# An LSTM step with one tanh for all four gates and its waits in another order, and the attention's output bias added behind the first two batches' sums

## The reference

```
h   = LSTM(norm(x)), 56 steps, 20 units:
      i, f, g, o = split(x_t @ W_ih.T + b_ih + b_hh + h @ W_hh.T)
      c = sigmoid(f) * c + sigmoid(i) * tanh(g)
      h = sigmoid(o) * tanh(c)
mu_w  = relu(h @ W_mu.T + b_mu);  sigma = sigmoid(h @ W_sig.T + b_sig)
mu_t  = mu_w[0] * mu_{t-1} + mu_w[1] / 56 + mu_w[2] * (t + 1) / 56
w     = exp(-(rel - mu)^2 / (2 sigma^2)), masked causally, normalised
x1    = x + w @ norm(x)
x2    = x1 + softmax(norm(x1) WQ (ctx WK)^T / 8) (ctx WV) WO + bO     16 heads of 64
out   = x2 + layer_norm(gelu(norm(x2) @ W1[e] + b1[e]) @ Wo + bo + norm(x2)) * gamma + beta, e = argmax of 4 router logits
```

## Time and profile before

| | |
|---|---|
| median of 3 executions | 1666.67 us (1659.07 to 1667.97) |
| profiled execution, its own time | 1670.2 us |
| its span in the trace | 1668.3 us |
| busy: TensorE, VectorE, ScalarE, GpSimd | 1539.9, 1169.3, 898.0, 805.3 us |
| LSTM, first input product to last head | 18.43 to 127.1 us |
| its 40 steps in the loop | 38.9 to 112 us |
| first scores | 162.28 us |

### The profile page before, as it was taken

The page is one execution under the profiler, slowest core; times in us unless marked ns, Lnnn a source line. Parts: engine busy times, 40 slices in busy tenths (PEclk is TensorE's granted clock), DMA queues, the critical chain, the costliest instruction groups (busy, mean ns, idle before and its releaser), DMA issues.

```text
span 1668.3 us, 25258 instructions
## 1 busy us (share of the span) xinstructions
PE 1539.9 (92%) x7555; PEld 1091.7 (65%) x7555; DVE 1169.3 (70%) x1870; ACT 898.0 (54%) x1281; POOL 805.3 (48%) x410
## 2 busy tenths in 40 slices
PE   6885999999999999999999999999999999989997
PEld 3345666676767676767666666666676767666574
DVE  4348777767676767686777777777767776868645
ACT  4234665555555555556565656565565555535311
POOL 2003365555555555555555555555555555536510
PEclk9996999999999999999999999999999999989898
DMA  4000000000000000000000000000000000000000
GB/s 154 26 9 10 1 37 38 38 37 37 37 37 26 37 25 37 25 37 33 37 37 37 37 37 37 37 37 37 37 37 37 37 37 37 38 5 14 1 1 22
DMA packets 15058, 54.91 MB, mean 33 GB/s; under 512 B 919, under 2 KB 6122, under 8 KB 15022
## 3 DMA queue, kind: packets, MB, share of 16 engines
q1 hardware_dynamic: 15022, 54.46, 8.6%
HBM read 53.54 MB, written 0.92 MB: 33 GB/s over the span
## 4 chain that ended last, share of the span: by engine, by line
PE 75%; DVE 12%; issue 5%; ACT 5%; POOL 1%; DVEq 1%; DMA 0%; POOLq 0%; ACTq 0%
PE ps L736 28%; PE ps L702 26%; PE ps L608 3%; PE ps L603 3%; DVE arena L1280 3%; PE ps L594 3%; PE ps L798 3%; DVE arena L1294 3%; PE ps L587 2%; PE ps L716 2%; ACT arena L996 2%; PE ps L523 1%; ACT ring L990 1%; POOL arena L456 1%; PE ps L724 1%
## 5 line engine op out<-in xcount | busy, mean ns | idle before, releaser
L456 POOL TENSOR_TENSOR arena<-arena,ring 125x896 f32<-125x896 f32 x192 | 426.0, 2219 | 17.5 <-POOL arena L456 0.5
L702 PE MATMUL ps<-q_hi,ctxT_hi 128*125 128x448 f32 x768 | 402.7, 524 | 32.7 <-ACT ring L990 26.7
L1280 DVE TENSOR_TENSOR arena<-arena,ps 125x896 f32<-125x896 f32 x336 | 363.1, 1081 | 89.6 <-PE ps L702 89.3
L456 POOL TENSOR_TENSOR arena<-arena 125x896 f32<-125x896 f32 x112 | 237.0, 2116 | 345.8 <-ACT arena L996 337.1
L990 ACT ACTIVATE ring<-ps 125x896 f32<-125x896 f32 x192 | 176.2, 918 | 380.2 <-DVE arena L1280 211.1
L736 PE MATMUL ps<-ring,ctx_nat 125*128 125x448 f32 x768 | 347.8, 549 | 0.0
L702 PE MATMUL ps<-q_hi,ctxT_lo 128*125 128x448 f32 x768 | 282.4, 368 | 0.0
L702 PE MATMUL ps<-q_lo,ctxT_hi 128*125 128x448 f32 x768 | 282.3, 368 | 0.0
L736 PE MATMUL ps<-arena,ctx_nat 125*128 125x448 f32 x576 | 243.6, 546 | 2.3
L702 PEld LDWEIGHTS ps<-q_hi,ctxT_hi 128*125 128x125 f32 x768 | 144.7, 188 | 104.7 <-issue 88.3
L1294 DVE TENSOR_TENSOR ring<-ring,ps 125x896 f32<-125x896 f32 x192 | 201.8, 1079 | 0.0
(11 more groups left out here) (203 smaller groups left out, 1936.4 us busy)
## 6 DMA issues: line engine op xcount, KB each, us to landing
ctx_raw<-in_ctx_dram SPq DMA_DIRECT2D x32, 750.0 KB
ctx_nat<-in_ctx_dram SPq DMA_DIRECT2D x32, 750.0 KB
w_sb<-in_L_ffn_W_dram SPq DMA_DIRECT2D x1, 1024.0 KB
resid<-in_x_dram SPq DMA_DIRECT2D x1, 896.0 KB, 5.9
out_dram<-ctx_raw SPq DMA_DIRECT2D x4, 224.0 KB, 2.5
ctx_raw<-in_L_xattn_WQ_dram SPq DMA_DIRECT2D x1, 512.0 KB
w_sb<-in_L_xattn_WK_dram SPq DMA_DIRECT2D x1, 512.0 KB
w_sb<-in_L_xattn_WV_dram SPq DMA_DIRECT2D x1, 512.0 KB
```

Of the source, the lines that this page charges most:

```text
L456: g.tensor_tensor(summed, chunk[0] if j == 1 else summed, chunk[j], ALU.add).then_inc(s["prob_added"], 1)
L702: m = mm(score_ps[j % 2][:, half, :], cx[k][:, rows], q[k][:, cols], start=(n == 0), stop=(n == 2))
L1280: v.tensor_tensor(run_max, kept(k, 0) if j == 1 else run_max, score_ps[j % 2], ALU.max).then_inc(s["maxed"], 1)
```

## The change

It has five parts. **One tanh.** Since sigmoid(z) = (1 + tanh(z / 2)) / 2, the weights and biases of gates i, f and o are halved when they are copied out of PSUM, and one tanh instruction covers all four gates (20 x 128). The tiles hold twice the cell and twice `h`; `W_hh` and the head's weights are halved once more for that, and the row of ones in `lstm_h` becomes 2. **Three VectorE instructions for four.** `cell` is now the fifth block behind the four gates, so one instruction computes (gate + 1) x (g or cell) for i and f together (20 x 64), a second adds the two parts, and a third makes `h`. **Waits.** VectorE's wait for its own earlier step now stands ahead of the wait for ScalarE. **Biases.** They are loaded as columns beside the weights (80, 80, 3 and 1 numbers of 4 bytes), behind the weights in the SP queue; TensorE's first transposes wait for all eight loads, and ScalarE makes seven copies instead of three. **GpSimd's order.** `bO` is added in two halves of eight tiles, behind the additions of batch 0 and of batch 1, and the heads of a pair wait for it; the three powers in period (14, 0) stand behind addition 11 together.

```diff
@@ sync
-            sp.dma_start(w_hh_in[0:4 * PE, :], W_hh).then_inc(s["lstm_w_in"], 16)
...
-            sp.dma_start(whhT[PE:PE + 1, :], b_ih.rearrange("(a n) -> a n", a=1)).then_inc(s["bias_in"], 16)
...
+            for column, bias in ((PE, b_ih), (PE + 1, b_hh)):
+                sp.dma_start(w_hh_in[0:4 * PE, column:column + 1], bias.rearrange("(n a) -> n a", a=1)).then_inc(s["lstm_w_in"], 16)
...
@@ gpsimd
-            g.memset(lstm_h, 1.0).then_inc(s["zeros_made"], 1)
+            g.memset(lstm_h, 2.0).then_inc(s["zeros_made"], 1)
...
-            need(pool, "ln_done", 2 * GROUPS)
-            g.tensor_tensor(resid_k, resid_k, bO_b[:, None, :].to_broadcast((TOK, PAIRS, D)), ALU.add).then_inc(s["bO_added"], 1)
...
-                    if isinstance(i, int) and i == PAIRS - 2 and k == 0 and j in POWERS_AT:
-                        power(3, POWERS_AT.index(j))
+                if isinstance(i, int) and i == 0:
+                    tiles = slice(k * PAIRS // 2, (k + 1) * PAIRS // 2)
+                    if k == 0:
+                        need(pool, "ln_done", 2 * GROUPS)
+                    g.tensor_tensor(resid_k[:, tiles, :], resid_k[:, tiles, :], bO_b[:, None, :].to_broadcast((TOK, PAIRS // 2, D)), ALU.add).then_inc(s["bO_added"], 1)
+                if isinstance(i, int) and i == PAIRS - 2 and k == 0:
+                    for q in range(GROUPS - 1):
+                        power(3, q)
@@ tensor
-            pe.wait_ge(s["lstm_w_in"], 64)
+            pe.wait_ge(s["lstm_w_in"], 128)
...
@@ scalar
-            a(cell_t, cell, ACT.Sigmoid).then_inc(s["table_loaded"], 1)
+            a(cell_t, cell, ACT.Tanh).then_inc(s["table_loaded"], 1)
...
+            for start, stop, half in ((0, 2 * PE, 0.5), (2 * PE, 3 * PE, 1.0), (3 * PE, 4 * PE, 0.5)):
+                a(wihT[:, start:stop], ps[:, 3, start:stop], ACT.Copy, scale=half).then_inc(s["lstm_w_sb"], 1)
+                a(whhT[0:PE + 2, start:stop], ps[0:PE + 2, 3, 128 + start:128 + stop], ACT.Copy, scale=half / 2).then_inc(s["lstm_w_sb"], 1)
...
-                    a(gate_act[:, 0:3, :], gates[:, 0:3, :], ACT.Sigmoid).then_inc(s["sig_ready"], 1)
-                    a(gate_act[:, 3, :], gates[:, 3, :], ACT.Tanh).then_inc(s["tanhg_ready"], 1)
-                    need(act, "cell_step", 3 * t + 3)
-                    a(cell_t, cell, ACT.Tanh).then_inc(s["tanhc_ready"], 1)
+                    a(gate_act[:, 0:4, :], gates, ACT.Tanh).then_inc(s["tanhg_ready"], 1)
+                    need(act, "cell_step", 2 * t + 2)
+                    a(cell_t, cell, ACT.Tanh, scale=0.5).then_inc(s["tanhc_ready"], 1)
@@ vector
-                    need(dve, "sig_ready", t + 1)
-                    need(dve, "cell_step", 3 * t)
-                    v.tensor_tensor(cell_f, gate_act[:, 1, :], cell, ALU.mult).then_inc(s["cell_step"], 1)
+                    need(dve, "cell_step", 2 * t)
                     need(dve, "tanhg_ready", t + 1)
-                    v.tensor_tensor(cell_i, gate_act[:, 0, :], gate_act[:, 3, :], ALU.mult).then_inc(s["cell_step"], 1)
-                    need(dve, "cell_step", 3 * t + 2)
-                    v.tensor_tensor(cell, cell_f, cell_i, ALU.add).then_inc(s["cell_step"], 1)
+                    v.scalar_tensor_tensor(cell_parts, gate_act[:, 0:2, :], 1.0, gate_act[:, 3:5, :], ALU.add, ALU.mult).then_inc(s["cell_step"], 1)
+                    need(dve, "cell_step", 2 * t + 1)
+                    v.scalar_tensor_tensor(cell, cell_parts[:, 1, :], 0.5, cell_parts[:, 0, :], ALU.mult, ALU.add).then_inc(s["cell_step"], 1)
                     need(dve, "tanhc_ready", t + 1)
-                    v.tensor_tensor(lstm_h[0:PE, u, :], gate_act[:, 2, :], cell_t, ALU.mult).then_inc(s["h_ready"], 1)
+                    v.scalar_tensor_tensor(lstm_h[0:PE, u, :], gate_act[:, 2, :], 1.0, cell_t, ALU.add, ALU.mult).then_inc(s["h_ready"], 1)
...
                     need(dve, "recip_done", 4 * (pair + 1))
+                    need(dve, "bO_added", 2)
...
-            need(dve, "bO_added", 1)
```

More of the change, by code:

```diff
@@ L134, in decoder_layer @@
         w_in = cut(D)
-        w_hh_in = cut(PE)
-        w_head_in = cut(PE)
+        w_hh_in = cut(PE + 2)
+        w_head_in = cut(PE + 1)
         wihT = cut(4 * PE)
@@ L139, in decoder_layer @@
         headT = cut(NB + 1)
-        gate_act = cut(4 * B, PE).rearrange("p (g b) -> p g b", g=4)
-        cell = cut(B, PE)
-        cell_f = cut(B, PE)
-        cell_i = cut(B, PE)
+        gate_act = cut(5 * B, PE).rearrange("p (g b) -> p g b", g=5)
+        cell = gate_act[:, 4, :]
+        cell_parts = cut(2 * B, PE).rearrange("p (g b) -> p g b", g=2)
         cell_t = cut(B, PE)
@@ L196, in decoder_layer @@
         s = {name: stack.enter_context(nc.semaphore("s_" + name)) for name in (
-            "x_in lstm_w_in bias_in attn_w_in ffn_w_in ctx_in0 ctx_in1 nat_in0 nat_in1 out_stored0 out_stored1 "
+            "x_in lstm_w_in attn_w_in ffn_w_in ctx_in0 ctx_in1 nat_in0 nat_in1 out_stored0 out_stored1 "
             "identity_made ones_made minus_made indices_made rel_made causal_made picks_made zeros_made "
@@ L200, in decoder_layer @@
             "ln_step ln_var rstd_done ln_done xT_ps xT_sb "
-            "gates_ready sig_ready tanhg_ready cell_step tanhc_ready h_ready head_ready head_read "
+            "gates_ready tanhg_ready cell_step tanhc_ready h_ready head_ready head_read "
             "sigma_done pick_ps picks_read gauss_step rows_picked gauss_diff gauss_sq gauss_arg gauss_exp gauss_ready gauss_w2 "
@@ L233, in decoder_layer @@
         PIECES = {"k": "mask", "x": "tokens", "l": "logits", "o": "onehot", "t": "turn", "s": "sums", "p": "project", "q": "query"}
-        POWERS_AT = (9, 10, 11)
         EARLY = 4
@@ L313, in _ @@
             sp.dma_start(w_in[0:4 * PE, :], W_ih).then_inc(s["lstm_w_in"], 16)
-            sp.dma_start(w_hh_in[0:4 * PE, :], W_hh).then_inc(s["lstm_w_in"], 16)
-            sp.dma_start(w_head_in[0:NB, :], W_mu).then_inc(s["lstm_w_in"], 16)
-            sp.dma_start(w_head_in[NB:NB + 1, :], W_sig).then_inc(s["lstm_w_in"], 16)
-            need(sp, "biased_cleared", 2)
-            sp.dma_start(headT[PE:PE + 1, 0:NB], b_mu.rearrange("(a n) -> a n", a=1)).then_inc(s["bias_in"], 16)
-            sp.dma_start(headT[PE:PE + 1, NB:NB + 1], b_sig.rearrange("(a n) -> a n", a=1)).then_inc(s["bias_in"], 16)
-            sp.dma_start(whhT[PE:PE + 1, :], b_ih.rearrange("(a n) -> a n", a=1)).then_inc(s["bias_in"], 16)
-            sp.dma_start(whhT[PE + 1:PE + 2, :], b_hh.rearrange("(a n) -> a n", a=1)).then_inc(s["bias_in"], 16)
+            sp.dma_start(w_hh_in[0:4 * PE, 0:PE], W_hh).then_inc(s["lstm_w_in"], 16)
+            sp.dma_start(w_head_in[0:NB, 0:PE], W_mu).then_inc(s["lstm_w_in"], 16)
+            sp.dma_start(w_head_in[NB:NB + 1, 0:PE], W_sig).then_inc(s["lstm_w_in"], 16)
+            for column, bias in ((PE, b_ih), (PE + 1, b_hh)):
+                sp.dma_start(w_hh_in[0:4 * PE, column:column + 1], bias.rearrange("(n a) -> n a", a=1)).then_inc(s["lstm_w_in"], 16)
+            sp.dma_start(w_head_in[0:NB, PE:PE + 1], b_mu.rearrange("(n a) -> n a", a=1)).then_inc(s["lstm_w_in"], 16)
+            sp.dma_start(w_head_in[NB:NB + 1, PE:PE + 1], b_sig.rearrange("(n a) -> n a", a=1)).then_inc(s["lstm_w_in"], 16)
             sp.dma_start(wq_raw, WQ).then_inc(s["attn_w_in"], 16)
@@ L484, in _ @@
             pe.wait_ge(s["identity_made"], 2)
-            pe.wait_ge(s["lstm_w_in"], 64)
+            pe.wait_ge(s["lstm_w_in"], 128)
             tr(ps[:, 3, 0:4 * PE], w_in[0:4 * PE, :], ident[0:4 * PE, 0:4 * PE])
-            tr(ps[0:PE, 3, 128:128 + 4 * PE], w_hh_in[0:4 * PE, :], ident[0:4 * PE, 0:4 * PE])
-            tr(ps[0:PE, 3, 256:256 + NB + 1], w_head_in[0:NB + 1, :], ident[0:NB + 1, 0:NB + 1]).then_inc(s["lstm_w_ps"], 1)
+            tr(ps[0:PE + 2, 3, 128:128 + 4 * PE], w_hh_in[0:4 * PE, :], ident[0:4 * PE, 0:4 * PE])
+            tr(ps[0:PE + 1, 3, 256:256 + NB + 1], w_head_in[0:NB + 1, :], ident[0:NB + 1, 0:NB + 1]).then_inc(s["lstm_w_ps"], 1)
             def turn_tokens(banks, count, q):
@@ L503, in _ @@
             pe.wait_ge(s["xT_sb"], 4)
-            pe.wait_ge(s["lstm_w_sb"], 3)
-            pe.wait_ge(s["bias_in"], 64)
+            pe.wait_ge(s["lstm_w_sb"], 7)
             pe.wait_ge(s["zeros_made"], 3)
@@ L880, in _ @@
             need(act, "zeros_made", 3)
[L881 removed]
+            a(cell_t, cell, ACT.Tanh).then_inc(s["table_loaded"], 1)
             act.wait_ge(s["lstm_w_ps"], 1)
             need(act, "biased_cleared", 2)
[L884 to L886 removed]
+            for start, stop, half in ((0, 2 * PE, 0.5), (2 * PE, 3 * PE, 1.0), (3 * PE, 4 * PE, 0.5)):
+                a(wihT[:, start:stop], ps[:, 3, start:stop], ACT.Copy, scale=half).then_inc(s["lstm_w_sb"], 1)
+                a(whhT[0:PE + 2, start:stop], ps[0:PE + 2, 3, 128 + start:128 + stop], ACT.Copy, scale=half / 2).then_inc(s["lstm_w_sb"], 1)
```

(1 more changed line is left out.)

3 lines of the change are left out of this document (removed).

## The result

The changed kernel takes **1660.56 us** (median of 20 runs, 1652.44 to 1666.13), the kernel before 1666.53 us beside it (20 runs, 1659.07 to 1672.92): a ratio of **0.9968, 95% interval 0.9955 to 0.9982**, 5.3 us faster by the ratio. 9.7 us were forecast. The time lies in the forecast's range (1650 to 1664), the gain is 0.32%, within the 0.5% that was called no change.

What follows compares the result with a forecast made beforehand. Gains were to come from the first 168 us, bound by the chain of waits: -5.4 + 0.3 - 3.1 - 1.5 = -9.7, 1670.2 to 1660.5 us (1657.0 from the median 1666.67). Range for all cases: 1650 to 1664.

Steps and rivals of the forecast that it cites:

- LSTM, -5.4: LSTM recurrence: 40 loop steps shorter by 0.125 us each, -5.0; last 8 steps -0.3; first iteration -0.1.
- waits 0.08: VectorE's waits in an LSTM loop step: the new order saves 0.08 us a step, -3.2 us over 40.
- the longer tanh: ScalarE in an LSTM step: one tanh over 128 elements takes 0.27 us, +0.03 a step.
- three instructions for four, -0.075: VectorE in an LSTM step: first product's start to the addition's start 0.245 us for 0.32, saving 0.075.
- from below: Larger LSTM gain: with the tanh at +0 and the waits at 0.09 a step, 6.9 us.
- Second table load, +0.3: ScalarE behind the last context copy: a 1283 ns load, mostly covered by VectorE's scan for mu, costs 0.3 us.
- Bias halves' own time, powers, columns, 0: GpSimd's halves (about 2.3 us each) fall into its pauses; moved powers and bias column loads also change nothing: 0.
- `q_lo`, -3.1: Ahead of the first scores: without GpSimd's addition beside it, `q_lo` takes 1.08 us for 4.30; scores start 3.1 us sooner.
- the held clock, -1.5: TensorE behind the first scores: its pause shrinks from 4.84 to 1.75 us, so full clock holds: -1.5 us.
- the clock falls anyway: Rival: TensorE's clock falls at the first scores despite the shorter pause; gain 8.2 us, 1658.5; chance 0.20.
- a drain beside the load: Second table load: the skill's rule adds a 1380 ns drain per switch; by it the sum would be 1.4 us higher.
- The half rate: Rival: VectorE's three LSTM scalar_tensor_tensor run at half rate, 6.2 us off the gain, 1663.2; chance 0.07.

Runs made afterwards that it cites:

- b1: Changed kernel with VectorE's two LSTM waits in the usual order, tanh first, then its own last step; 1663.95 us, ratio 0.9975 to the kernel before.
- c1: Kernel before with VectorE's first two LSTM waits exchanged, own last step ahead of the sigmoid; 1663.53 us, ratio 0.9984.
- c3: Changed kernel with the gates' tanh in two activations (three gates and one); 1661.42 us, ratio 0.9971 to the kernel before.
- a2: Kernel before with only the output bias added in two halves behind the first two batches' sums; 1667.96 us, ratio 0.9997.
- a4: Changed kernel with a sigmoid as first activation, so one table load serves both functions; 1660.75 us, ratio 0.9964 to the kernel before.
- a3: Kernel before with only the third LayerNorm's three powers moved behind the eleven additions of their batch; 1667.96 us, ratio 1.0001.
- b2: Kernel before with only the four biases loaded as columns ahead of the weights' transposes; 1669.26 us, ratio 1.0017.
- a1: Kernel before with the LSTM part alone (one tanh, three VectorE instructions, wait order, bias columns); 1660.34 us, ratio 0.9965.
- b3: Changed kernel with ten copies of 1024 elements on VectorE ahead of the first LayerNorm; 1666.41 us, ratio 0.9998 to the kernel before.
- b4: Changed kernel with sixteen extra matmuls of 448 columns in TensorE's wait for the third LayerNorm; 1663.21 us, ratio 0.9979 to the kernel before.
- c2: Kernel before with one more wait, for both `q_lo`, ahead of GpSimd's whole output bias addition; 1665.51 us, ratio 0.9982.
- c4: a4 with the waits of the 32 batches ordered so that the one ending last stands last; 1658.00 us, ratio 0.9944 to the kernel before.

## Why the prediction was right, and where it was not

**What came and what didn't.** The forecast gave 0.68 to a gain above 0.5% and 0.29 to one within it, and the second came: 5.3 us by the ratio, 3.0 to 7.5, for 9.7. That the time of 1660.56 stands beside the forecast's 1660.5 is luck: that sum starts from one execution of 1670.2 us, and the 20 runs beside the change have their median at 1666.53. Taken from the median the forecast was 1657.0, 3.6 too low.

**LSTM, -5.4: right.** The 40 steps fell from 73.4 to 68.3 us without half clock in them, 5.1, for -5.0. Its parts were sized otherwise: "waits 0.08" is 0.09 a step (b1, c1), one tanh is worth 0.05 (c3), where the longer tanh was charged at +0.03, and three instructions for four, -0.075, nothing beside c1. The case "from below" was added up wrong: with the tanh at +0 and the waits at 0.09 it gives 7.3 (40 x 0.165, 8 x 0.075 and 0.1), not 6.9; nothing hung on it. The first iteration is bound by TensorE as said, 1.96 us a step in both; its 1.1 us in the profiled pair go with the moment at which TensorE's matmuls get shorter. TensorE's step matmuls still took 0.58 us at 25.60 before, 0.41 us at 24.70 after, and in the traces of other kernels the change to 0.41 came anywhere from 21 us to behind 29 us (a2).

**Second table load, +0.3: right** (+0.2 by a4). **Bias halves' own time, powers, columns, 0: right** within 1 us (a3, b2), and the halves lie in GpSimd's pauses.

**`q_lo`, -3.1, and the held clock, -1.5: right for one kind of execution, and this is the step that was sized wrong.** For the execution that was profiled the places were right: 59.22 to 54.39 us, -4.8 for -4.6. But there are two kinds. From the table load to the first addition:

| `q_lo` that is caught | traces | us |
|---|---|---|
| the first; half clock for 6.8 us ahead of the scores | before | 59.22 |
| the second; half clock for 3.4 us there | a1, a3, b2, c1 | 55.6 to 55.7 |
| none; 3.4 us | a4, b3, b4, c2 | 53.3 |
| none; 6.8 us | after, a2, b1 | 54.4 to 54.5 |
| none; 6.8 us, other waits in the batches | c4 | 55.1 |
| none; 6.8 us, and 3.4 us more behind the first scores | c3 | 56.3 |

The clock ahead of the scores decides, and not the 0.14 us. In all eight traces with half clock for 3.4 us there the query products take 5.45 us, the first `q_lo` starts 0.13 to 0.15 us ahead of the place where the whole addition starts or would start (0.08 us behind the last `xnorm`), and TensorE's pause in front of the scores is 0.63 us. In all six with 6.8 us the products take 6.2 to 6.9, and `q_lo` starts 1.0 to 1.3 us behind that place, so there the whole addition would catch it. The pause of 1.7 us that was forecast belongs to this kind. Moving the addition is worth 4.8 us in it (59.22 to 54.4) and 2.3 in the other (55.6 to 53.3). The forecast priced the first kind for all executions; with the addition in its old place four traces of five are of the other one. How often each comes among the runs that were not profiled is not known. At equal clock, where the fall itself is taken out, a2 gives 2.4 and c2 3.2.

**Where the rest went: the clock.** At equal clock the change is worth 9.4 us. That this is close to the 9.7 is in part luck: the loop's 5.1 and the 2.3 to 4.8 of `q_lo` make 7.4 to 9.9, less 0.2 for the table. But the changed kernel's runs have a mean clock of 0.9769 against 0.9789 (102 runs of before): 0.0020 by 1.27 us for each 0.001 is 2.5 us, and leaves some 7, within the measured 3.0 to 7.5. The lower clock seems to go with the bias addition, not with the LSTM: kernels with the whole addition in its old place have 0.9788 (150 runs of before, a1, a3, b2 and c1), those with it moved 0.9775 (101 runs, b4 left out, which warms TensorE; 0.9777 with it), a difference of four standard errors, 1.8 us. The grouping was made behind the runs, so this is a hint and not shown; if it holds, most of the halves' 2.3 us is given back in this way, and a2, whose ratio allows 4 us either way, measures no change. The rival "the clock falls anyway" (0.20, 1658.5) had the right currency: c3 shows that fall behind the first scores, the changed kernel's trace doesn't.

What stays open: why moving an addition of 4.5 us at 156 us would lower the mean clock. The longer fall ahead of the scores (five of nine traces with the addition moved have it, one of five with it in its old place) begins before the addition would, so it may be chance; these shares would make some 0.0004 of the 0.0013 (an estimate: 0.36 x 3.4 us at half, of 1660). One trace can't say how much of the tail's belongs to the change, and the changed kernel's runs were measured apart from those of the experiments. That falls in the tail don't need the change is shown by a3, with the LSTM of before and the addition in its old place: 24 us at half clock and a tail of 123.2 us. The deepest (0.84) are in traces with the addition moved, c2 with the LSTM of before among them.

Of the Trainium skill's rules that were weighed, "ScalarE: Activation LUTs" § What ACT_TABLE_LOAD costs gives a drain beside the load, by which the sum would have been 1.4 us higher; the trace has the activation 0.02 us behind a load of 1.28 us, and a4 finds 0.2 us. The half rate of the Trainium skill's "Vector Engine (DVE) Microarchitecture Reference" § Points that are easy to get wrong was the rival at 0.34 us; the 64-element instruction takes 0.214 us and the 32-element ones 0.180, about 1 ns for each further element, as the tensor_tensor of the earlier trace rows does. The trace doesn't agree with the half rate.

## What to carry to other kernels

Where waits are against values that a loop works out, put the wait that ends last directly in front of the instruction; look in the chain of waits for a queue's piece (DVEq, ACTq, PEq) between a finished producer and its consumer. Two lines exchanged gave seven tenths of the loop's gain, and the same rule elsewhere took 4.6 us off 25 batches and made the kernel with the lowest median (1658.00). Before pricing a collision of two engines from a trace, ask what brought each of them there at that moment: here a clock fall of 3.4 or 6.8 us ahead of it moved one by 1.1 to 1.4 us, and one trace shows one side. And where the clock moves the time by more than the change does, compare at equal clock as well.

## What was not expected of the hardware

- A register instruction behind the late wait cost VectorE about 0.09 us each time (3.5 and 3.6 us over 40 steps, b1 and c1): 0.12 us from the tanh's end (60.92) to the product (61.04) in b1, 0.01 to 0.02 in the changed kernel.
- The granted clock fell to half with TensorE busy throughout (12.00 of the 12.00 us ahead of it, 22.00 of 22.00 in it, at 0.53), and a tail of equal work took 115.6 to 125.8 us for it.
- Beside GpSimd's addition `q_lo` took 4.32 us for 1.09 when it started second, and the addition 5.41 for 4.52 us when it did.
- Matmuls of 448 fp32 columns took 0.76 us each in a row of sixteen (12.19 us, b4), in two instructions each.
